# A hand-ordered two-layer transformer kernel: start-up loads placed behind the first stacks, banks released by their readers' own signals, lookup masks and copies merged

## The reference, cut to what matters

```
x = layernorm(x + attn0(x));  x = layernorm(x + ffn0(x))
x = layernorm(x + attn1(x));  x = layernorm(x + ffn1(x))      # x: (4, 256, 256)

attn0: 32 query heads, 8 key/value heads, head size 8;   softmax(q k^T / sqrt(8)) v, then Wo
attn1: 16 query heads, 8 key/value heads, head size 16
ffn0:  w = float8_e4m3(w) for gate (256x768), up (256x768), down (768x256), each with an output scale
       down(silu(gate(x)) * up(x))
ffn1:  w = lut[idx], a table of 16 floats looked up by int32 indices, for gate, up (688x256), down (256x688)
       down(silu(gate(x)) * up(x))
```

## Time and profile before

| | us |
|---|---|
| median of 3 runs (lowest, highest) | 373.83 (372.24, 374.71) |
| the profiled execution's own time | 374.77 |
| its span, first to last instruction | 373.0 |
| TensorE busy | 304.6 (82%) |
| VectorE busy | 267.1 (72%) |
| ScalarE busy | 249.3 (67%) |
| GpSimd busy | 188.8 (51%) |
| mean granted TensorE clock | 0.91 of full |

### The profile page before, as it was taken

One profiled execution on the slowest core, in us unless ns is written; L12 is line 12 of the kernel. 1 busy time (PEld: TensorE's weight loads), 2 busy tenths in 40 slices (PEclk: granted clock), 3 DMA queues, 4 the chain that ended last, 5 costly groups with the idle time before them and its releaser, 6 DMA issues.

```text
span 373.0 us, 7419 instructions
## 1 busy us (share of the span) xinstructions
PE 304.6 (82%) x2608; PEld 198.0 (53%) x2608; DVE 267.1 (72%) x464; ACT 249.3 (67%) x449; POOL 188.8 (51%) x261
## 2 busy tenths in 40 slices
PE   8517126766789997798988899999999999999991
PEld 7413001222424553265544565577667688879990
DVE  7627898999787889889889689668762675416251
ACT  3725857888759866687678976875668746653440
POOL 5715835141454236755567622763465236638663
PEclk9956555799959998999999999999999999999996
DMA  6994433100410000014003200292003100000000
GB/s 185 316 192 115 130 89 91 44 26 25 121 37 26 25 26 21 7 35 121 6 22 87 69 1 4 71 255 69 1 4 102 28 3 2 8 23 29 3 30 28
DMA packets 24876, 23.09 MB, mean 62 GB/s; under 512 B 3543, under 2 KB 24839, under 8 KB 24839
## 3 DMA queue, kind: packets, MB, share of 16 engines
q1 hardware_dynamic: 24838, 22.61, 21.7%
HBM read 10.47 MB, written 3.26 MB: 37 GB/s over the span
## 4 chain that ended last, share of the span: by engine, by line
PE 63%; ACT 9%; DVE 8%; issue 7%; SPq 5%; POOL 4%; DMA 3%; POOLq 0%; ACTq 0%; DVEq 0%
PE FB L1197 15%; PE PV L1141 10%; PE FB L1210 8%; PE MM L1086 7%; ACT PB L814 5%; PE FB L1169 4%; PE SC L1116 4%; PE SC L1121 4%; DVE MX L923 3%; DMA QS<-QP 3%; PE FB L1041 3%; SPq L515 2%; PE FB L1065 2%; PE FB L1152 2%; PE FB L1060 2%
## 5 line engine op out<-in xcount | busy, mean ns | idle before, releaser
L923 DVE TENSOR_REDUCE MX<-MM 128x4 f32<-128x1024 f32 x96 | 117.2, 1221 | 32.7 <-PE MM L1086 28.4
L814 ACT ACTIVATE PB<-SC 128x1024 f32<-128x1024 f32 x96 | 98.3, 1024 | 35.0 <-PE SC L1116 21.6
L1086 PE MATMUL MM<-KS,QS 62*128 62x256 bf16 (+1 forms) x384 | 48.4, 298 | 29.7 <-DVE MX L923 29.1
L679 POOL TENSOR_TENSOR HL<-HF,HH 128x256 fp32r<-128x256 f32 (+1 forms) x48 | 35.6, 749 | 61.1 <-ACT HH L790 60.7
L1141 PE MATMUL PV<-PB,VP 128*32 128x256 f32 x768 | 62.3, 408 | 2.2 <-ACT PB L814 2.2
L1086 PEld LDWEIGHTS MM<-KS,QS 62*128 62x128 bf16 (+1 forms) x384 | 18.8, 98 | 60.6 <-DVE MX L923 40.4
L1010 DVE COPY_PREDICATED LV<-LB,LV 128x432 f32<-128x432 uint8 x70 | 46.5, 724 | 4.1 <-ACT LV L862 2.6
L1197 PE MATMUL FB<-XH,W 128*128 128x256 f32 x192 | 43.5, 308 | 0.2 <-DVEq L953 0.2
L1197 PE MATMUL FB<-XL,W 128*128 128x256 f32 x192 | 38.5, 282 | 0.1
L1116 PE MATMUL SC<-QS,KS 64*128 64x256 bf16 x256 | 27.7, 299 | 11.0 <-ACT PB L814 9.5
L971 DVE SCALAR_TENSOR_TENSOR AA<-TH,FB 128x256 f32<-128x256 f32 (+1 forms) x48 | 19.9, 415 | 20.1 <-ACT TH L805 12.7
(11 more groups left out here) (94 smaller groups left out, 575.7 us busy)
## 6 DMA issues: line engine op xcount, KB each, us to landing
QS<-QP SPq DMA_DIRECT2D x48, 128.0 KB, 2.5
IX<-in_idx SPq DMA_DIRECT2D x10, 216.0 KB, 2.6
dw<-LO SPq DMA_DIRECT2D x10, 216.0 KB, 1.9
W1L<-dw SPq DMA_DIRECT2D x10, 216.0 KB, 4.0
KS<-KP SPq DMA_DIRECT2D x24, 64.0 KB, 2.0
XT<-in_xt SPq DMA_DIRECT2D x4, 256.0 KB, 3.5
X<-in_x SPq DMA_DIRECT2D x4, 256.0 KB, 7.1
out<-X SPq DMA_DIRECT2D x4, 256.0 KB, 2.1
```

Source lines behind the costliest of these rows:

```text
L679: pool.tensor_tensor(HL[0:r, i, :], HF[0:r, c % 2, :], HH[0:r, i, :].bitcast(F32), ALU.subtract).then_inc(h_parts, 1)
L814: act.activation(PB[:, quad % PB_QUADS, kt, :, :], SC[:, :, :], ACT.Exp, scale=DH[layer(j)] ** -0.5).then_inc(exp_done, 1)
L923: dve.tensor_reduce(mx, MM[:, :, :].rearrange("p (f i) s -> p f i s", f=2), axis=AX.X, op=ALU.max).then_inc(max_red, 1)
L1086: ins = pe.matmul(MM[:, 2 * f + i, :], QS[lo:lo + r, j % NST, qs + h, qt * P:(qt + 1) * P], keys(j)[lo:lo + r, j % NST, ks, :], start=True ...
```

## The change

It computes the same, with six kinds of edits.

1. **Loads.** SyncE issues the layer 1 weights, Wo, the residual x and the tokens of batches 2 and 3 behind the stacks of job 0, spread between later stacks.
2. **Bank release.** TensorE waits for the reader's own semaphore (`h_new`, `m_parts`, `turned`, `normed`) where there is one; the separate increments and the waits ahead of them are gone on ScalarE and VectorE. VectorE's `gu` step no longer waits for its second instruction but at the start of the next `gu`.
3. **Lookup.** The four masks of a chunk are one VectorE instruction with the two inputs IB and BITS (a constant), and `lut2`, `lut3` are one predicated copy each, with a mask repeated by a zero step.
4. **fp8 mask.** BIG is made of the bytes that ScalarE wrote (Q8B), as 96 words in place of 384; VectorE now waits for ScalarE's rounding, and ScalarE's next chunk waits for the mask (`big_done`).
5. **Waits.** TensorE drops waits that an earlier wait already covers. The transposing matmul of `mt` loads 128 columns in place of 32 or 64, from a tile with zeros behind them (two memsets more at the start, and four for BITS).
6. **Orders.** All five lists are rewritten; of SyncE's one line is shown.

```diff
@@ bank release
-            uses[bank] += 1
-    return fill
+            prior[fill_of(step)] = held[bank]
+            held[bank] = fill_of(step)
+            uses[bank] += step[0] in COUNTED
+    return fill, prior
...
+        def wait_bank(pe, step):
+            if step[0] == "gu":
+                pe.wait_ge(h_new, 6 * step[1] + step[2] + 1)
+            elif step[0] == "mt":
+                pe.wait_ge(m_parts, 2 * step[1] + step[2] + 1)
+            elif step[0] == "turn":
+                pe.wait_ge(turned, 2 * step[1] + step[2] + 1)
+            elif step[0] == "back":
+                pe.wait_ge(normed, 2 * step[1] + step[2] + 1)
+            else:
+                wait_free(pe, step)
...
                     act.activation(ON[:, p, :], bank[:, 0:S], ACT.Copy).then_inc(normed, 1)
-                    act.wait_ge(normed, 2 * j + p + 1)
-                    act.sem_inc(fill_free[slot], 1)
...
@@ VectorE, gu
+                    if 6 * j + i >= 1:
+                        dve.wait_ge(h_new, 6 * j + i)
...
-                    link(dve.scalar_tensor_tensor(out=HF[0:r, (6 * j + i) % 2, :], in0=bank[0:r, S:2 * S],
-                                                  scalar=c, in1=AA[0:r, :], op0=ALU.mult, op1=ALU.mult))
-                    dve.sem_inc(h_new, 1)
-                    dve.sem_inc(fill_free[slot], 1)
+                    dve.scalar_tensor_tensor(out=HF[0:r, (6 * j + i) % 2, :], in0=bank[0:r, S:2 * S], scalar=c,
+                                             in1=AA[0:r, :], op0=ALU.mult, op1=ALU.mult).then_inc(h_new, 1)
@@ VectorE, q8
-                    dve.wait_ge(ld_raw[c % 2], 16 * (c // 2 + 1))
+                    dve.wait_ge(q8_bytes, c + 1)
...
-                    link(dve.tensor_scalar(BIG[:, :], RAW[:, c % 2, :].bitcast(I32), 0x40000000, None,
-                                           ALU.bitwise_and))
+                    dve.tensor_scalar(BIG[:, :].bitcast(I32), Q8B.bitcast(I32), 0x40404040, None,
+                                      ALU.bitwise_and).then_inc(big_done, 1)
@@ VectorE, lookup
-                    for k in range(4):
-                        ins = dve.tensor_scalar(LB[:, k, :].bitcast(I32), src, 0x01010101 << k, None,
-                                                ALU.bitwise_and)
-                    ins.then_inc(bit_done, 1)
+                    w = LUT_W // 4
+                    dve.tensor_tensor(LB[:, :, :].rearrange("p k w -> p (k w)").bitcast(I32).rearrange("p (k w) -> p k w", k=4),
+                                      src.rearrange("p (o w) -> p o w", o=1).broadcast_to((P, 4, w)),
+                                      BITS[:, :].rearrange("p (k o) -> p k o", o=1).broadcast_to((P, 4, w)),
+                                      ALU.bitwise_and).then_inc(bit_done, 1)
...
-                    for i in range(0, LUT // 2, 2 * gap):
-                        ins = dve.copy_predicated(LV[:, i, :], LB[:, k, :], LV[:, i + gap, :])
-                    link(ins)
+                    pairs = LUT // 4 // gap
+                    mask = LB[:, k:k + 1, :].broadcast_to((P, pairs, LUT_W)) if pairs > 1 else LB[:, k:k + 1, :]
+                    ins = dve.copy_predicated(LV[:, 0:LUT // 2:2 * gap, :], mask, LV[:, gap:LUT // 2:2 * gap, :])
@@ TensorE, mt
-                        ins = pe.matmul(bank[0:h, qt * P:(qt + 1) * P],
-                                        MS[:, m % 2, qt, 0:halves(j), :, :].rearrange("q f a h -> q (f a h)"),
-                                        IDB[:, :], start=True, stop=True)
+                        ins = pe.matmul(bank[:, qt * P:(qt + 1) * P], MS[:, m % 2, 32 * qt:32 * qt + P], IDB[:, :],
+                                        start=True, stop=True)
@@ one line of SyncE's list
-        "load.0 ldxt.1 ldq8.0 ldq8.1 ldix.0 ldix.1 ldxt.2 load.1 load.2 ldx.0 ldx.1 ldx.2 ldxt.3 ldx.3 ldix.2 "
+        "ldxt.1 ldq8.0 ldq8.1 ldix.0 ldix.1 load.0 ldix.2 qstack.0.1 qstack.0.0 qstack.0.2 ldq8.2 kstack.0.0 ...
```

87 lines of the change are left out of this document (54 added, 33 removed), and 238 rows, old and new, of the table ORDER.

## The result

| | before | after |
|---|---|---|
| median of 4 runs (lowest, highest), us | 373.91 (372.24, 374.71) | 362.22 (361.44, 363.92) |
| the profiled execution's own time | 374.77 | 362.06 |
| its span | 373.0 | 360.2 |

The medians differ by 11.7 us. Ratios leave out executions that took over 1.5% more than the fastest of the same kernel. The prediction said 358, 16 us faster, in a range from 349 to 368.

What follows compares the result with a forecast made beforehand. TensorE's work plus its gaps was taken as the bound, VectorE bounding the gaps from 30 to 90 us. Terms 5.5 + 7.0 + 1.5 + 2.0 = 16.0 us off 374.8 gave 358.8, as median 358 us, range 349 to 368.

Steps and rivals of the forecast that it cites:

- The two regimes: Before 210 us TensorE has gaps, together 59.2 us; from 210 to 360 us its work alone sets the time.
- the full stretch: From 210 to 360 us, TensorE busy 149.0 of 150 us; no change of length expected.
- The start, 5.5 us: Loads moved behind job 0's stacks bring the first maximum from 28.66 to about 23 us: 5.5 us, ends 2.5 and 7.
- VectorE's work, 7.0 us: Merged lookup copies and masks and a smaller fp8 mask: 10.6 us less VectorE work, 7.0 us of time, ends 0 and 11.
- there I keep 0.8: Share of saved VectorE work counted as time before 90 us, where its busy share is 0.92; later 0.5.
- sign of being wrong: The prediction would be wrong if lookup copies of 1728 elements took 2.2 us or more.
- The lock between VectorE and GpSimd: Within the slower rival (0.07): a shared port pair locked per instruction, so a 1.95 us copy holds GpSimd longer than 0.55.
- The masks: Merging a lookup chunk's four VectorE masks: 1.2 us less work, ends -1.5 and +2.4; no gain undisturbed.
- Bank release, 1.5 us: Waits after `gu` steps, 8.0 us, one third before 210 us, half of that on the path: 1.5 us, ends 0 and 4.
- Orders, 2 us: Job 4's projections move ahead of job 1's transpose into TensorE's gap: 2 of 3.5 us; other moves unpriced, -6 to +6.
- the absorbed head start: Rival, chance 0.12: only the start's lower end and half of VectorE's term arrive, 6.5 us in all: 367 us.
- run into its suppliers: Slower rival, chance 0.07: VectorE's lookup, listed earlier, stands until GpSimd and ScalarE have made the candidates: 378 us.

Runs made afterwards that it cites:

- thin lookup: The changed kernel with the lookup's predicated copies on 16 of 432 columns, so ffn1's weights are wrong: 358.47 us, ratio 0.9594 to the kernel before.

## Why the prediction was right, and where it was not

**The structure held.** The two regimes are there, the full stretch kept its length (mt.3.1 to mt.7.1 107.1 us, before 108.2), and nearly all of the gain lies ahead of it. The sum's total is 4 us too large. The idle time ahead of the full stretch fell to 51.9 us and not to the 43 that was forecast; 4.9 us came by a higher granted clock, which the sum did not have.

**The start, 5.5 us: the step right, the follow-up wrong.** I wrote that VectorE is the bound right behind the start and has its work earlier. The first reduction came 7.0 us sooner, more than the 5.7 worked out (the queries' stack was issued at 11.90 and not 12.4). But I followed the stack only up to the first maximum and never read what TensorE does between the first and the second. Alone the step gave nothing; in the new kernel 3.4 us. "The displaced loads are due late" was false for the tokens of batches 2 and 3, and the low clock made their projections long: 413 to 448 ns a matmul, where eight of this shape took 1.95 us, 244 ns each, at 11 us.

**VectorE's work, 7.0 us: the size of the work nearly right, its worth wrong.** VectorE is busy 258.1 us, 256 was said. The copies are 2.10 and 1.12 undisturbed for 1.95 and 1.05 said, the masks 0.59 for 0.61 and 0.20 as said. The copies saved 3.9 us and not 7.0, and two steps made the difference. I took the price per element from two other instructions, 1.04 ns; from the two merged copies it is 1.13 ns, so that merging saves 0.12 and 0.04 us a chunk undisturbed, 1.6 us in ten chunks and not 3.8. And the disturbances fell from some 6.4 to 4.1 us, which is 2.3 and not 3.2 (the merged copies average 2.20 and 1.23, the single ones 0.83 for 0.63). The mean of 2.20 us reaches the 2.2 that the prediction had named as a sign of being wrong; in this term it was wrong. The larger error is the step "there I keep 0.8", and the 0.5 behind it. It took a busy share of 0.92 as proof of a bound. In an engine that works off a list the share tells how much is in it, not whether the engine that it alternates with would come sooner. Measured were 2.7 us for the 5.6 us that the three edits take off in the new lists (VectorE busy 263.7 with the old ones), and 4.7 for 32.7 in the thin lookup. Whether the first few microseconds are dearer than the rest is open: both numbers have an uncertainty of over 2 us, and the masks' 5.4 us (3.1 in the total) were worth nothing that could be measured.

**The lock between VectorE and GpSimd** was named in a rival with no row for GpSimd's side. There is one now: the 2.58 us above, and the normalisation of X on GpSimd, which takes 597 ns on average before, 655 with the copies unmerged and 693 in the change. The Trainium skill ("SBUF — State Buffer", Who interferes with whom) has an exclusive lock on a shared port pair for a whole instruction; these rows agree. The change's ten copies of 1728 elements show more: a GpSimd operation on two elements that started 0.11 us behind a copy took 2.00 us (0.19 elsewhere), and two copies that started 0.44 and 0.46 us into a GpSimd operation of some 1.15 us took 2.64 us and not 2.10. Three others that started 0.14 to 0.41 us into an operation of 0.56 to 0.72 us took 2.09 or 2.10, which the rule alone does not explain. Not shown is what the lock costs in time: with the copies unmerged GpSimd's normalisation is faster and the kernel is not.

**The masks.** The Trainium skill ("VectorE: DVE Perf Modes", The perf-mode tier table) gives a 32-bit operation with one input in SBUF twice the rate of one with two. The rows agree: four instructions of 108 words take 0.58 us undisturbed, one of 432 takes 0.59, no gain; and the time shows none (0.9693 with the old masks, 0.9719 with the new). In VectorE's own busy time the merge does save, 7.6 us against 13.0 in the same lists. One start in place of four that can be disturbed is the likely reason, not tested; in the lists of before the same forty masks took only 8.4 us.

**Bank release, 1.5 us: three times too small.** I had two rows, 8.0 us, took a third of them and half of that. The same table of the kernel before had more waits for the same instruction, by the next `gu` step, the split of the maxima and the copies, which I did not add (3.8, 1.0 and 0.6 us); and the third was worked out by counting `gu` steps, though those before 210 us stand in the in-order lists of three engines that alternate, where a delay is passed on. Measured 4.8 us with 2.4 of uncertainty, part of it perhaps the collision shown above. The dropped waits and the wider load of `mt`, which I cost at nothing, were not run alone: the code edits together are worth 6.3 us in the new lists (0.9888 against 0.9719), VectorE's and the release 2.7 and 4.8, so nothing is left for them within the uncertainty.

**Orders, 2 us: too small.** The piece that I priced moved as said: job 4's projections run some 17 us sooner, and the idle time from 90 to 160 us is 9.7 us for 12.1. But what I said I could not price is the larger part: the orders other than the start are worth 3.8 us with the new code and 5.9 with the old one. Which of the moved steps carry it is open. The parts do not add up, and need not: start, VectorE and release, each taken back from the change, make 3.4 + 2.7 + 4.8 = 10.9 us, already the whole 10.5, because each contains what it gives only together with the lists. In the old kernel each gives less: nothing for the start, 3.3 us for all of the code.

**So the total was near partly by luck:** two terms too large by 2.1 and 4.3 us, two too small by 3.3 and by 1.8 or more, and the sum took the parts as independent, which they are not. Of the rivals, the absorbed head start was true in part, but not for its reason (job 1's stacks): the lead of 7.0 us at the first reduction is 2.9 at the second, because of the projections between the two. The lookup did not run into its suppliers: VectorE's wait ahead of the copies went from 4.1 to 3.5 us.

## What to carry to other kernels

- An engine that alternates with others in written lists need not be the bound though it is busy 90% of a stage. Before pricing its work, read the step from one turn to the next and what ends the gap in it; better, thin the work in an experiment.
- When a transfer is moved forward, read the receiving engine's list up to its *second* turn, and ask of every displaced load who waits for it first. A start gained by the transfers alone can be worth nothing until the consumer's list is changed with it.
- When edits and orders change together, run both halves alone and a few parts taken back. Parts that depend on one another have no single price, and what is left over after subtracting some of them is not the price of the rest.
- A semaphore released by an instruction of its own, behind a wait for the result, delays all that stands behind it on that engine. Add up every wait that names that instruction, the small ones on its own engine too.

## What the hardware showed that I had not expected

- The time goes with the granted clock by as much as with an edit. Of 38 executions of the kernel before, the four with a mean granted clock of 0.925 or more took 371.6 us on average, the eight with 0.905 or less 374.3. Where the lower level comes differs between kernels that do the same work in slightly shifted time: 0.54 from 100 to 110 us before, 0.52 from 70 to 80 with the code edits alone, and in the change nothing under 0.69 in any slice of 10 us between 60 and 350.
- A GpSimd operation on two elements a partition took 2.58 us when it began 0.06 us behind a VectorE copy of 2.10 us, and 0.72 when it began 0.14 us ahead of one.
- A predicated copy with its mask repeated by a zero step costs no more per element than a plain one: 1728 elements in 2.10 us, 864 in 1.12, 432 in 0.63.
